# A causal attention and feed-forward layer on one core: V transposes in the output rows' banks, an earlier high part, and later rows as one, two, one tile

## The reference, cut to what matters

```python
# x: (1, 1024, 512); 32 query heads, 8 key/value heads, head size 128; all float32
q, k, v = x @ wq, x @ wk, x @ wv          # split into heads; q and k get rotary embedding
scores = q @ k.T / sqrt(128)              # causal mask, softmax over keys
out = softmax(scores) @ v                 # 4 query heads share one k and v
x = layernorm(x + concat(out) @ wo)
nx = x * rsqrt(mean(x * x) + 1e-5) * ln_w
x = layernorm(x + (silu(nx @ gate_w.T) * (nx @ up_w.T)) @ down_w.T)   # inner size 1792
```

## Time and profile before

| | |
|---|---|
| median of three runs | 1179.38 us (1178.23 to 1181.88) |
| profiled execution, its own time | 1179.82 us |
| its span, first to last instruction | 1178.0 us |
| TensorE busy | 1119.9 us, 95% |
| GpSimd, VectorE, ScalarE busy | 832.1 (71%), 811.7 (69%), 620.8 us (53%) |
| mean granted TensorE clock | 0.996 of full speed |

### The profile page before, as it was taken

How to read it: one execution, slowest core, us unless ns; L and a number is a source line. 1 busy time by engine, 2 the same in 40 slices (tenths; PEclk the granted TensorE clock), 3 DMA queues, 4 the chain that set the end, 5 groups by cost and what they waited for, 6 DMA issues and landing times.

```text
span 1178.0 us, 18687 instructions
## 1 busy us (share of the span) xinstructions
PE 1119.9 (95%) x5346; PEld 939.7 (80%) x5346; DVE 811.7 (69%) x1416; ACT 620.8 (53%) x1122; POOL 832.1 (71%) x544
## 2 busy tenths in 40 slices
PE   8799999999999999999999999999997699999997
PEld 6578878887888788878888887888775588888885
DVE  6788777877886887788778877777878742222224
ACT  4565656665665666565655565566655332122224
POOL 3589977987897799779978996898675343343431
PEclk9999999999999999999999999999999899999999
DMA  6755555655565566566556655665555401111101
GB/s 191 210 149 152 135 139 141 161 138 139 140 161 129 149 156 156 129 151 156 148 130 153 156 129 138 152 155 134 130 129 127 128 19 53 54 53 53 53 0 72
DMA packets 148346, 148.75 MB, mean 126 GB/s; under 512 B 15200, under 2 KB 128864, under 8 KB 148320
## 3 DMA queue, kind: packets, MB, share of 16 engines
q1 hardware_dynamic: 148320, 148.43, 49.2%
HBM read 37.23 MB, written 2.10 MB: 33 GB/s over the span
## 4 chain that ended last, share of the span: by engine, by line
PE 63%; POOL 14%; DVE 8%; issue 8%; DMA 3%; ACT 1%; SPq 1%; DVEq 0%; POOLq 0%; ACTq 0%
PE ACC L1053 13%; PE ACC L1055 13%; PE ACC L1054 13%; PE S L1053 4%; PE S L1055 4%; PE S L1054 4%; PE S L1069 4%; PE S L1071 4%; PE S L1070 4%; POOL qk_raw L476 4%; POOL PT_lo L502 3%; POOL rope_s L477 3%; DVE turned L804 2%; POOL Q_lo L486 2%; DMA rope_s<-qk_raw 2%
## 5 line engine op out<-in xcount | busy, mean ns | idle before, releaser
L596 ACT ACTIVATE probs<-S,neg_max 128x128 f32<-128x128 f32 (+7 forms) x256 | 189.3, 740 | 266.6 <-DVE neg_max L793 266.5
L793 DVE CUSTOM_DVE_ANT_0 S<-S,mask 128x128 f32<-128x128 f32 (+7 forms) x256 | 194.4, 759 | 157.8 <-PE S L1071 157.2
L502 POOL TENSOR_TENSOR PT_lo<-PT_lo,PT_hi 128x896 fp32r<-128x896 f32 (+2 forms) x97 | 203.1, 2094 | 114.2 <-ACT PT_hi L603 114.2
L804 DVE STREAM_TRANSPOSE turned<-probs 128x128 f32<-128x128 f32 (+7 forms) x256 | 197.7, 772 | 3.2 <-ACT probs L596 3.2
L863 DVE SCALAR_TENSOR_TENSOR y<-ACC,row_rcp,y 128x512 f32<-128x512 f32 x256 | 177.6, 732 | 21.8 <-PE ACC L1055 21.8
L603 ACT ACTIVATE PT_hi<-PT_lo 128x1024 fp32r<-128x1024 f32 (+3 forms) x160 | 165.0, 1031 | 17.8 <-DMA PT_lo<-turned 17.1
L1053 PE MATMUL ACC<-PT_hi,V_hi 128*128 128x512 f32 (+3 forms) x384 | 135.0, 351 | 24.7 <-DVE PT_lo L811 10.2
L476 POOL TENSOR_TENSOR qk_raw<-qk_raw,cos_sb 128x512 f32<-128x512 f32 x76 | 124.3, 1636 | 35.9 <-DMA rope_s<-qk_raw 35.4
L554 POOL TENSOR_TENSOR PT_lo<-rope_s,PT_hi 128x512 fp32r<-128x512 f32 x28 | 36.2, 1293 | 155.8 <-ACT PT_hi L732 155.8
L1069 PE MATMUL S<-K_hi,Q_hi 128*128 (+5 forms) x384 | 132.7, 345 | 7.7 <-POOL Q_lo L486 4.2
L1054 PE MATMUL ACC<-PT_lo,V_hi 128*128 128x512 f32 (+3 forms) x384 | 133.9, 349 | 0.0
(11 more groups left out here) (128 smaller groups left out, 2574.9 us busy)
## 6 DMA issues: line engine op xcount, KB each, us to landing
PT_lo<-turned SPq DMA_DIRECT2D x256, 128.0 KB, 2.6
PT_lo<-turned SPq DMA_DIRECT2D x128, 208.0 KB, 3.7
rope_s<-qk_raw SPq DMA_DIRECT2D x160, 128.0 KB, 2.8
PT_lo<-turned SPq DMA_DIRECT2D x128, 112.0 KB, 2.5
PT_lo<-turned SPq DMA_DIRECT2D x128, 96.0 KB, 2.4
wq_raw<-in_L_attn_wq_dram SPq DMA_DIRECT2D x32, 256.0 KB, 2.9
wkvo_raw<-in_L_attn_wo_dram SPq DMA_DIRECT2D x32, 256.0 KB, 2.7
turned<-in_L_ffn_gate_w_t_dram SPq DMA_DIRECT2D x7, 512.0 KB, 4.0
```

Of the source, the lines that this page charges most:

```text
L502: nc.gpsimd.tensor_tensor(lo, lo.bitcast(F32), hi.bitcast(F32), ALU.subtract).then_inc(pt_lo_done[half], 1)
L596: nc.scalar.activation(dst, src, ACT.Exp, bias=neg_max[:, at:at + 1], scale=-1.0, accum_out=row_sum[:, j % 2, i:i + 1]).then_inc(exp_done, 1)
L793: nc.vector.tensor_tensor_reduce(src, src, bias, scale=1.0, scalar=MASKED, op0=ALU.add, op1=ALU.min, accum_out=neg_max[:, at:at + 1]).then ...
L804: nc.vector.transpose(dst.rearrange("p b (r i) -> p r b i", i=QB), src.rearrange("p (r b i) -> p r b i", b=4, i=QB)).then_inc(turn_done, 1)
```

## The change

Three edits. First, the two V transposes of a group's first head move from steps 5 and 6 to steps 3 and 4. They no longer take a bank of the ring (now counted by `ring`, apart from `x`) but banks 1 and 3, in the rows' turn: TensorE counts them as two more `y`, they wait for the add that frees the bank (`y_free`) and for the copy of V, and VectorE's `V_lo` raises `y_free` when it is done. The third transpose of each raises `y_done`, so that the rows' counts go on. The first `pv` of a group waits for the second `V_lo`. Second, ScalarE makes the high part of tiles 2 and 3 (`pt_high(1)`) ahead of step 5's exponential instead of behind it. Third, the later rows of a head are multiplied as tile 4 in step 5, tiles 5 and 6 in step 6 and tile 7 in step 7, where they were 4 and 5 in step 6, and 6 and 7 in step 7.

```diff
@@ Tally.PER
+        "ring": REP * 4 + 4,
-        "split": REP * 2 + 2,
-        "y": REP * NT,
+        "split": REP * 2,
+        "y": REP * NT + 2,
+        "turned_v": 2,
@@ extras
     if i == 5:
-        return [("q", 1, j + 1, 0, NC)] * (j + 1 < heads) + [("vt", 0, j, 0, HT)] * (j % REP == 0)
-    if i == 6 and j % REP == 0:
-        return [("vt", 1, j, 0, HT)]
+        return [("q", 1, j + 1, 0, NC)] * (j + 1 < heads)
-    if i == 3 and j > 0:
-        return [("pv", 1, j - 1, 0, HT)]
+    if i == 3:
+        return [("pv", 1, j - 1, 0, HT)] * (j > 0) + [("vt", 0, j, 0, HT)] * (j % REP == 0)
     if i == 4:
-        return [("pv", 1, j - 1, HT, NT)] * (j > 0)
+        return [("pv", 1, j - 1, HT, NT)] * (j > 0) + [("vt", 1, j, 0, HT)] * (j % REP == 0)
@@ row_tiles
-    return {1: [0, 1], 2: [2, 3], 6: [4, 5], 7: [6, 7]}.get(i, []) if j > 0 else []
+    return {1: [0, 1], 2: [2, 3], 5: [4], 6: [5, 6], 7: [7]}.get(i, []) if j > 0 else []
@@ ScalarE, split_high: V's source
-                    dst, src = V_hi[:, half * HT:(half + 1) * HT, :].rearrange("p a b -> p (a b)"), ACC[:, bank]
+                    dst, src = V_hi[:, half * HT:(half + 1) * HT, :].rearrange("p a b -> p (a b)"), ACC[:, 1 + half * 2]
@@ ScalarE, step
+                if i == HIGH_AT[1][0]:
+                    pt_high(1, n["head"])
                 if not (last and (j, i) == LAST_STEPS[-1]):
                     exponent(j + (i + 1) // NT, (i + 1) % NT)
...
-                    if i == step_of and j >= ago:
+                    if i == step_of and j >= ago and k != 1:
@@ VectorE, split_low
+                if kind == "vt":
+                    hi, lo = [a[:, half * HT:(half + 1) * HT, :].rearrange("p a b -> p (a b)") for a in (V_hi, V_lo)]
+                    nc.vector.tensor_tensor(lo, ACC[:, 1 + half * 2], hi.bitcast(F32), ALU.subtract).then_inc(y_free, 1)
+                    n.add("turned_v")
+                    n.add("y")
+                    return
@@ TensorE, other
-                bank = n.n["x"] % 2 * 2
+                bank = 1 + half * 2 if kind == "vt" else n.n["ring"] % 2 * 2
+                if kind == "vt":
+                    pe.wait_ge(copy_done, n.marked(("v", half)))
+                    pe.wait_ge(y_free, n["y"] + (ADDS_BEFORE - 1))
...
+                        if k == HT - 2:
+                            last.then_inc(y_done, 1)
...
+                        if k == 0 and half == 0 and head % REP == 0:
+                            pe.wait_ge(y_free, n.marked(("vt", 1)) + ADDS_BEFORE)
```

More of the change, by code:

```diff
@@ L619, in copy_out @@
                 act_e.wait_ge(x_done, n["x"] + 1)
-                dst, src = qk_raw[:, n.n["rope"] % 2], ACC[:, n.n["x"] % 2 * 2]
+                dst, src = qk_raw[:, n.n["rope"] % 2], ACC[:, n.n["ring"] % 2 * 2]
                 if kind == "v":
@@ L629, in copy_out @@
                 n.add("x")
+                n.add("ring")
             def split_high(kind, half):
                 act_e.wait_ge(x_done, n["x"] + 1)
-                bank = n.n["x"] % 2 * 2
                 if kind == "pv":
-                    dst, src = by_query(O_hi, half), by_block(bank)
+                    dst, src = by_query(O_hi, half), by_block(n.n["ring"] % 2 * 2)
+                    n.add("ring")
                 else:
-                    dst, src = V_hi[:, half * HT:(half + 1) * HT, :].rearrange("p a b -> p (a b)"), ACC[:, bank]
+                    dst, src = V_hi[:, half * HT:(half + 1) * HT, :].rearrange("p a b -> p (a b)"), ACC[:, 1 + half * 2]
                 nc.scalar.activation(dst, src, ACT.Copy).then_inc(split_hi_done, 1)
@@ L746, in pair @@
                     weight_high(p + 1, 1)
-            y_base = HEADS * NT
+            y_base = HEADS * NT + GROUPS * 2
             act_e.wait_ge(eps_done, 1)
@@ L839, in split_low @@
             def split_low(kind, half, head):
[L841 to L845, removed]
-                    hi, lo = [a[:, half * HT:(half + 1) * HT, :].rearrange("p a b -> p (a b)") for a in (V_hi, V_lo)]
-                    src = ACC[:, bank]
-                nc.vector.tensor_tensor(lo, src, hi.bitcast(F32), ALU.subtract).then_inc(split_done, 1)
-                n.add("x")
+                dve.wait_ge(split_hi_done, n["split"] + n["turned_v"] + 1)
+                if kind == "vt":
+                    hi, lo = [a[:, half * HT:(half + 1) * HT, :].rearrange("p a b -> p (a b)") for a in (V_hi, V_lo)]
+                    nc.vector.tensor_tensor(lo, ACC[:, 1 + half * 2], hi.bitcast(F32), ALU.subtract).then_inc(y_free, 1)
+                    n.add("turned_v")
+                    n.add("y")
+                    return
+                hi, lo = [by_query(a, half) for a in (O_hi, O_lo)]
+                nc.vector.tensor_tensor(lo, by_block(n.n["ring"] % 2 * 2), hi.bitcast(F32),
+                                        ALU.subtract).then_inc(split_done, 1)
+                n.add("ring")
                 n.add("split")
-                if kind == "pv":
-                    reciprocals(head, half)
+                reciprocals(head, half)
             def reciprocals(head, half):
@@ L903, in _ @@
             nc.vector.memset(eps_rms[:], RMS_EPS * LN_EPS).then_inc(y_free, ADDS_BEFORE)
-            n.add("x", len(START))
+            n.add("ring", len(START))
             for j, i in FIRST_HEAD:
@@ L1075, in other @@
             def other(kind, half, head, begin, end, start=False):
-                bank = n.n["x"] % 2 * 2
+                bank = 1 + half * 2 if kind == "vt" else n.n["ring"] % 2 * 2
                 acc, count = ACC[:, bank], products(kind, half)
-                if begin == 0 and ("bank", bank) in n.marks:
+                if kind == "vt":
+                    pe.wait_ge(copy_done, n.marked(("v", half)))
+                    pe.wait_ge(y_free, n["y"] + (ADDS_BEFORE - 1))
+                elif begin == 0 and ("bank", bank) in n.marks:
                     pe.wait_ge(copy_done if n.marks["bank", bank][0] == "copy" else split_done, n.marked(("bank", bank)))
@@ L1115, in other @@
                 n.add("x")
+                if kind == "vt":
+                    n.add("y")
+                    n.mark((kind, half), "y")
+                    return
+                n.add("ring")
                 released = "copy" if kind in "qkv" else "split"
@@ L1118, in other @@
                 n.mark(("bank", bank), released)
+                if kind in ("pv", "v"):
+                    n.mark((kind, half), released)
                 if kind == "pv":
-                    n.mark((kind, half), released)
                     n.add(f"pv{half}")
```

## The result

| | before | changed kernel |
|---|---|---|
| median of nine runs | 1179.49 us (1178.23 to 1181.88) | 1184.7 us (1183.41 to 1185.53) |
| ratio, with its 95% interval | | 1.0035 (1.0026 to 1.0045) |
| profiled execution, its own time | 1179.82 us | 1183.53 us |
| its span | 1178.0 us | 1181.7 us |

What follows compares the result with a forecast made beforehand. TensorE, busy 95% of the span, was taken as the bound. Fourth heads +3.2, second and third -0.5, first +0.4, last +0.4 and elsewhere 0 made +3.5 on the 1179.4 us median: 1182.9 us, range 1174 to 1191.

Steps and rivals of the forecast that it cites:

- The new wait, 0.46 us: Row tile 4 in step 5 waits for `O_lo` in all heads, 0.46 us each; seven fourth heads give +3.2 us.
- Second and third heads, -0.5: In 14 heads the wait before `pv` half 0 goes, the `O_lo` wait comes: 0.05 us less each at most.
- First heads, +0.4: Of seven first heads of a group, four win about 0.35 us and three lose 0.6: +0.4 us in all.
- three effects: V transposes: `V_lo` wait goes (1.3 us), transposes before s cost 0.8 us, the 0.26 us `O_lo` wait passes to row tile 4.
- Last head, +0.4: Tile 7's scores stand behind the `O_lo` wait, some 2.6 us later on VectorE: between 0 and +2.6, taken as +0.4 us.
- Elsewhere, 0: Extra register instructions on VectorE and TensorE, heads before the loop and the feed-forward part add 0.
- those for right: 25 or more `O_lo` waits, none before `pv` half 0, about 20 us before half 1, fourth stretch near 24.2 us.
- those for wrong: Waits before `pv` half 1 near 10 us; GpSimd's sum 1.3 us and `pt_low(2)` over 2.9; first heads below 21.5.
- this end stays where it is: `pt_low(4)` hangs on the rotary swap's transfer, ending 21.25 us after s, the start of step 5's first scores matmul.
- Slower still, the order at the shared access flips: GpSimd's sum goes ahead of VectorE's `pt_low(2)` in step 0, about 9 of 21 stretches: +9, 1192 us; chance 0.20.
- Faster, the last race is won: `pt_low(4)` gets ahead of GpSimd's `Q_lo`, first heads win 1.15 us each, 8 in all: 1175 us; chance 0.15.
- The new wait costs nothing: `O_lo` comes 0.4 us earlier, or the chain holds `pv` half 1 in fourth heads too: 1179.4 us; chance 0.10.

Runs made afterwards that it cites:

- `O_lo` ahead: The changed kernel with VectorE making `O_lo` and step 5's reciprocals ahead of the maximum of tile 6: 1179.74 us, ratio 1.0004.
- V and H: The changed kernel with its later rows as two and two again, the moved transposes and early high part kept: 1177.65 us, ratio 0.9978.
- H: The kernel before with only the earlier high part of tiles 2 and 3: 1177.07 us, ratio 0.9980.
- R: The kernel before with only the later rows as one, two, one: 1187.75 us, ratio 1.0060.
- V: The kernel before with only the V transposes moved into the rows' banks: 1180.72 us, ratio 1.0002.

## Why the prediction was right, and where it was not

The forecast was 1182.9 us, slower at the bound; it came to 1184.7. Its sum was +3.5 for the profiled execution, and the spans differ by 3.7. That it came so near is in part luck: against their measures first heads were put 0.6 too high and second and third 0.3, the fourth 0.2 too low, the last head 0.8 and the rest 0.2, and these nearly cancel. The 1.5 us by which the medians moved more than the spans stand in no trace. Term by term:

- *The new wait, 0.46 us:* right. 0.33 us to the start, 0.10 of refill, and 0.04 more over the next matmuls; the fourth head's stretch grew by 0.48, seven heads give +3.4 for +3.2. Shown by `O_lo` ahead, which takes it out (23.73).
- *Second and third heads, -0.5:* the total is near, -0.8, but it does not come from where the step had it. In the loop the stretch is TensorE's own again and as long as before, 21.49: `PT_lo` ends 0.06 before `pv` half 1 in V and H, whose mean is 21.19, but at s + 21.06 in head 13's stretch of the changed kernel, 0.43 ahead of the matmul. All of the 0.8 is won in heads 29 and 30, 0.4 in each. There TensorE has less to do and the chain ends the stretch: `pt_low(4)` ends at s + 20.96 and 20.92, where it ended at 21.38 and 21.36, since GpSimd's first product starts at s + 11.18 and 11.16 instead of 11.68 and 11.74. H takes 0.24 us out of two heads of four (21.49 to 21.25) and R spends it all. That H is worth nothing beside R the prediction implied; that it is worth 2.4 us without R stands in none of its sentences.
- *First heads, +0.4:* nearly right, 7 x (0.85 - 0.88) = -0.2. Two of its three effects hold: the wait for `V_lo` goes and the transposes cost 0.8 before s. The step that failed is "The wait for `V_lo` is thus spent on the wait for `pt_low(4)`, which grows from 1.1 to near 3 us", with its total of about 20 us of waits for VectorE's `PT_lo`. That total is 5.1 us, once, in the last head. The chain does end the stretch, as the step had it: in the first heads of the loop `pv` half 1 starts 0.05 to 0.06 us after `pt_low(4)` ends. But TensorE spends its free time earlier: scores of tile 4 wait 1.39 us for GpSimd's `Q_lo`, the row of step 2 waits 0.37 for the add `y`, and what is left before `pv` half 1 is too short to be printed. And it is 1.8 us as printed (1.39 and 0.37), not 3, because the chain in first heads got shorter: it ends at s + 21.03 to 21.08, where the step had 21.2 to 21.5.
- *Last head, +0.4:* mis-sized; it measured 1.2. The bounds held (0 to 2.6). The later maximum of tile 7 was counted, at 2.6 us; it starts 4.45 later after s (915.11 - 906.47 = 8.64, where it was 908.54 - 904.35 = 4.19). The fall of the granted clock to 0.51 was not counted; what that fall itself is worth is left open, since taking its first cause away brought 0.3 us within the noise.
- *Elsewhere, 0:* +0.2, of which +0.4 behind the last head, +0.1 before s of head 0, and -0.3 between `pv` half 1 and the next s.

Of its own signs, three of those for right came: 31 waits for `O_lo`, none before `pv` half 0, a fourth stretch of 24.21. One did not: 5.1 us of waits before `pv` half 1 instead of 20. And one of those for wrong came: first heads below 21.5 (21.12), though its own sum has 21.2 to 21.5 there. So the sum held, and its account of the first heads only in part. One assumption under both fails: "this end stays where it is". `pt_low(4)` no longer hangs on the swap's transfer but on `wo_lo`, as the next paragraph shows.

*Slower still, the order at the shared access flips:* it did not, by a margin of 0.14 us. In head 13's stretch of the changed kernel, GpSimd's operations around VectorE's `pt_low(2)`:

```profile
414.36 1.30 POOL L456 TENSOR_TENSOR wo_lo<-wkvo_raw,wo_hi 128x512 fp32r<-128x512 f32 x1 [3.31 <-ACT wo_hi L609]
415.61 1.31 POOL L476 TENSOR_TENSOR qk_raw<-qk_raw,cos_sb 128x512 f32<-128x512 f32 x1
...
418.12 1.73 DVE L814 TENSOR_TENSOR PT_lo<-PT_lo,PT_hi 128x1536 fp32r<-128x1536 f32 x1
418.26 2.74 POOL L480 TENSOR_TENSOR qk_raw<-qk_raw,rope_s 128x512 f32<-128x512 f32 x1
```

Against the earlier trace rows, counted from s, `pt_low(2)` comes 0.53 us later (s + 13.75 for 13.22) and the sum 0.24 earlier (s + 13.89 for 14.13), and VectorE is still first. The rival put both 7.1 us behind the maximum of tile 7, which is 1.16 later (s + 6.86 for 5.70), so that ScalarE's `wo_hi` and GpSimd's `wo_lo` are too. The sum came at +7.03, as it said, because the product starts at the end of `wo_lo`, s + 11.24; `pt_low(2)` came at +6.89. Its argument against itself, that the transfer is late in most stretches, did not hold: in 20 of the 21 first to third heads from head 4 on the product starts at the end of `wo_lo`, s + 11.16 to 11.27, where it started between s + 10.81 and 11.74 before. So what kept the order was 0.14 us, finer than the prediction could tell, and its outcome is luck. In first heads the order did turn, the other way. In head 12's stretch of the kernel before, GpSimd's sum went ahead:

```profile
389.01 1.29 POOL L480 TENSOR_TENSOR qk_raw<-qk_raw,rope_s 128x512 f32<-128x512 f32 x1
...
390.23 1.73 DVE L811 TENSOR_TENSOR PT_lo<-PT_lo,PT_hi 128x1536 fp32r<-128x1536 f32 x1
```

Now VectorE, without the two `V_lo` of its steps 6 and 7, is first:

```profile
391.19 1.78 DVE L814 TENSOR_TENSOR PT_lo<-PT_lo,PT_hi 128x1536 fp32r<-128x1536 f32 x1
...
391.44 2.69 POOL L480 TENSOR_TENSOR qk_raw<-qk_raw,rope_s 128x512 f32<-128x512 f32 x1
```

So it is in all seven first heads from head 4 on: GpSimd first in each before, VectorE in each now. In the experiments, too, VectorE is first there in every kernel with V and GpSimd in every one without.

*Faster, the last race is won:* the mechanism is real and its 1.15 us was sized right (1.18 against 2.31 us above), but the changed kernel's `pt_low(4)` still meets GpSimd's `Q_lo`, in first heads too, and takes its 2.2 us. What V wins in first heads goes with the order of `pt_low(2)` above; no run parts that order from the 1.3 us of `V_lo` that V also takes out of VectorE's way. *The new wait costs nothing:* fell, there are 31 waits and the fourth head shows each.

## What to carry to other kernels

When a unit of work is moved to fill a gap, compare when its operand is ready in every round of the loop with when the engine gets there: row tile 4 was put 0.2 us ahead of its operand, and that cost more than the other two edits won, most plainly in the one head of four where the engine had no wait to cover it. Moving the operand's producer first takes the loss away, but can have a price of its own: beside V and H it cost 3.7 us, and the runs leave open why. Try the parts of a change singly: one of three carried the loss, and the smallest of them alone beat the whole.

## What the runs showed of the hardware

- The same wait costs differently by its place. `O_lo` ends at s + 4.19 in second to fourth heads. Row tile 4 starts at s + 4.32 where the wait stands on a register instruction of the loop, and at s + 4.24 to 4.25 in the last group, which is written out: 0.13 us against 0.05 after the same event. The cause isn't settled: without V, second heads in the loop show s + 4.32 too, but third and fourth ones s + 4.25. And `pv` half 1 has it the other way round: where it waits for `pt_low(4)` it starts 0.05 to 0.06 us after its end in the loop and 0.14 to 0.16 in the last group.
- TensorE's granted clock fell to 0.51 in the 5 us in which it came back from 2.81 us without work, and stayed at 1.00 there after 1.45 us. With the last head's rows as two and two it fell to 0.50 around a later wait of 3.77 us.
- Two instructions that meet at the shared access are decided by 0.05 us of start, and the loser pays the whole of the other's time (1.18 against 2.31 us for the same subtraction).
